# Flamingo block on one core: the drain of attention and GpSimd's queue reordered, the experts' bias added by VectorE

## The reference

```
x = x + tanh(g_xattn[0]) * cross_attention(layernorm(x), ctx)    # 32 q heads, 8 kv heads, head size 128, q and k rms-normed
x = x + tanh(g_ffn[0])   * per_head_ffn(layernorm(x))            # t = x[:, perm]; 16 heads: gelu(t_h @ up_h) @ down_h; inverse perm
x = x + tanh(g_xattn[1]) * group_attention(layernorm(x), ctx)    # att = sum(p * g) per group and block scales t; group norm; + ctx
x = x + tanh(g_ffn[1])   * routed_experts(layernorm(x))          # 8 experts 512 -> 512 with bias, each token takes its argmax expert
```

## Time and profile before

| | us |
|---|---|
| median of three runs | 793.2 |
| the three runs | 792.78, 793.2, 797.03 |
| the profiled execution | 797.66 |
| its span, first to last instruction | 795.9 |
| PE busy in the span | 755.1 (95%) |
| DVE, ACT, POOL busy | 459.6, 430.5, 274.5 |
| mean granted clock of PE | 0.982 of full |

### The profile page before, as it was taken

The page is one execution under the profiler, slowest core; times in us unless marked ns, Lnnn a source line. Parts: engine busy times, 40 slices in busy tenths (PEclk is TensorE's granted clock), DMA queues, the critical chain, the costliest instruction groups (busy, mean ns, idle before and its releaser), DMA issues.

```text
span 795.9 us, 12734 instructions
## 1 busy us (share of the span) xinstructions
PE 755.1 (95%) x3975; PEld 592.2 (74%) x3975; DVE 459.6 (58%) x1038; ACT 430.5 (54%) x1274; POOL 274.5 (34%) x431
## 2 busy tenths in 40 slices
PE   5999989899999999999999999999999987987997
PEld 3888877788888888888888888888887743555775
DVE  4786411556465656564655565656558764787652
ACT  4543315556556556555655655655555466557831
POOL 0331005234334233424423523433322438624242
PEclk9999999999999999999999999999999999797999
DMA  8545461132041140140131203203142135664232
GB/s 303 180 133 172 133 189 46 49 150 76 15 173 37 57 173 28 54 183 15 66 119 80 66 30 158 80 15 120 34 131 85 54 109 184 240 261 158 73 109 76
DMA packets 42126, 87.82 MB, mean 110 GB/s; under 512 B 5561, under 2 KB 26041, under 8 KB 38226
## 3 DMA queue, kind: packets, MB, share of 16 engines
q1 hardware_dynamic: 38884, 78.71, 28.7%
q0 software_dynamic: 3184, 8.41, 3.1%
HBM read 70.28 MB, written 35.57 MB: 133 GB/s over the span
## 4 chain that ended last, share of the span: by engine, by line
PE 71%; DVE 6%; ACT 3%; POOL 2%; DMA 2%; issue 1%; POOLq 0%; DVEq 0%; SPq 0%
PE banks L882 8%; PE banks L916 7%; PE banks L884 7%; PE banks L883 7%; PE banks L918 7%; PE banks L917 7%; PE banks L868 6%; PE banks L903 3%; PE banks L895 2%; PE banks L1831 2%; PE banks L1830 2%; PE banks L1832 2%; PE banks L927 2%; PE banks L929 2%; PE banks L928 2%
## 5 line engine op out<-in xcount | busy, mean ns | idle before, releaser
L592 ACT ACTIVATE p_sb<-p_sb,nmax 128x128 f32<-128x128 f32 x256 | 99.7, 391 | 62.7 <-DVE nmax L784 62.5
L587 ACT ACTIVATE oT_hi<-banks 128x512 fp32r<-128x512 f32 x64 | 38.2, 597 | 140.1 <-PE banks L929 140.1
L822 DVE SCALAR_TENSOR_TENSOR x_sb<-banks,tgates,x_sb 128x512 f32<-128x512 f32 x64 | 48.0, 749 | 70.8 <-PE banks L918 70.8
L690 POOL TENSOR_TENSOR v_lo<-v_raw,v_hi 128x128 fp32r<-128x128 f32 x64 | 29.5, 461 | 133.6 <-ACT v_hi L635 133.6
L779 DVE SCALAR_TENSOR_TENSOR p_sb<-banks,q_rstd,mask 128x128 f32<-128x128 f32 x256 | 71.5, 342 | 4.5 <-POOL q_rstd L83 4.0
L868 PEld LDWEIGHTS banks<-kT,qT_sb 128*128 128x128 f32 x512 | 67.7, 193 | 5.9 <-issue 0.5
L695 POOL TENSOR_TENSOR p_sb<-p_sb,rsum 128x512 f32<-128x512 f32 x64 | 66.5, 1040 | 15.2 <-DVE rsum L812 15.2
L868 PE MATMUL banks<-kT,qT_sb 128*128 128x128 f32 x512 | 68.2, 277 | 0.1
L768 DVE TENSOR_TENSOR oT_lo<-banks,oT_hi 128x512 fp32r<-128x512 f32 x64 | 44.1, 689 | 33.0 <-ACT oT_hi L587 33.0
L400 PE MATMUL banks<-w_hi,ctx_hi 128*128 128x512 f32 x128 | 54.1, 422 | 9.0 <-DVE ctx_lo L331 9.0
L816 DVE TENSOR_TENSOR pT_lo<-banks,pT_hi 128x512 fp32r<-128x512 f32 x64 | 44.2, 690 | 24.9 <-ACT pT_hi L610 24.9
(11 more groups left out here) (276 smaller groups left out, 1901.9 us busy)
## 6 DMA issues: line engine op xcount, KB each, us to landing
sorted_x<-in_empty SPq DMA_DIRECT2D x8, 2064.0 KB, 9.7
w_raw<-in_wq_l SPq DMA_DIRECT2D x8, 1024.0 KB, 5.1
w_raw<-in_wo_l SPq DMA_DIRECT2D x8, 1024.0 KB, 4.8
exp_w<-in_exp_w_l SPq DMA_DIRECT2D x8, 1024.0 KB, 9.3
kT_scr<-kT_st SPq DMA_DIRECT2D x16, 256.0 KB, 2.3
v_scr<-v_st SPq DMA_DIRECT2D x16, 256.0 KB, 2.3
xs<-sorted_x SPq DMA_DIRECT2D x15, 258.0 KB, 2.8
v_raw<-v_scr SPq DMA_DIRECT2D x14, 256.0 KB, 2.6
```

What stands on the lines that cost most here:

```text
L592: last = act.activation(p_sb[:, b % 2, h * P:(h + 1) * P], p_sb[:, b % 2, h * P:(h + 1) * P], ACT.Exp, bias=nmax[:, b % 2, h:h + 1], accum ...
```

## The change

1. In the drain PE does the first nine matmuls of the output projection (`o_first`, heads 0 to 2), then the values of the next unit, then the last three (`o_last`). `transpose_x` stands behind `o_last`. oT_hi and oT_lo become double buffers. The z product of block 4 moves from `middle` into step 65, ahead of `o_first`(63). The order on DVE and ACT stays.
2. On GpSimd all eight `scale_ctx` run before the second four gathers, once the shift of the second normalisation is known; then all twelve scatters follow without a break, then the clearing and `recycled`.
3. ACT loads the Gelu table before the second normalisation, not behind the copies of transposed x. PE's waits for those copies move from pack 0 to pack 1.
4. The bias is loaded broadcast (2 MB, `s.bias`), and DVE adds gate * bias to the row in each tile (`add_bias`, between `split_x` and `add_y`, with the expert's number read by DVE from t = 8). The bias matmul, the zeros, the splits and the stores of the bias go.
5. The remaining 16 chunks of weights are split three a tile, from tile 0 on.

```diff
@@ attention
-        oT_hi = m.sb("oT_hi", [P, D], F32R)
-        oT_lo = m.sb("oT_lo", [P, D], F32R)
+        oT_hi = m.sb("oT_hi", [P, 2, D], F32R)
+        oT_lo = m.sb("oT_lo", [P, 2, D], F32R)
...
             def oT_split(u, b, g, odd):
                 act.wait_ge(pv_done, u + 1)
-                reached(act, o_done, u)
-                act.activation(oT_hi[:, :], oT_ps[:, :], ACT.Copy).then_inc(oT_hi_done, 1)
+                reached(act, o_done, u - 1)
+                act.activation(oT_hi[:, b % 2, :], oT_ps[:, :], ACT.Copy).then_inc(oT_hi_done, 1)
...
+            def o_first(u, b, g, odd):
                 pe.wait_ge(oT_lo_done, u + 1)
                 reached(pe, acc_done, u - 1)
                 if after(u, b, g, B - 3):
                     pe.wait_ge(s.z_copied[1], 2)
+                o_heads(u, b, g, odd, range(HG - 1))
+
+            def o_last(u, b, g, odd):
+                o_heads(u, b, g, odd, (HG - 1,)).then_inc(o_done, 1)
...
+            def z4(u, b, g, odd):
+                if after(u, b, g, B - 1):
+                    pe.wait_ge(pT_lo_done, UNITS)
+                    z_product(4)
...
-                [(scores, 0), (sum_squares, 4), (z01, 0), (p_transpose, -1), (z2, -1), (o_proj, -2),
-                 (transpose_x, -4), (values, -1), (z3, -1)])
+                [(scores, 0), (sum_squares, 4), (z01, 0), (p_transpose, -1), (z2, -1), (z4, -2), (o_first, -2),
+                 (values, -1), (o_last, -2), (transpose_x, -4), (z3, -1)])
@@ middle, ACT
+            act.wait_ge(xseed_done, 2)
+            act.preload_act_table(ACT.Gelu)
             act.wait_ge(xshift_done, 1)
             normalise2(5)
             normalise2(7)
             copy_xT(5)
             copy_xT(7)
-            act.preload_act_table(ACT.Gelu)
@@ middle, GpSimd
                 if c:
                     pool.wait_ge(ctx_nat_ld, 16)
+                    pool.wait_ge(xshift_done, 1)
                     pool.wait_ge(col_step, 2)
-                    scale_ctx(range(2))
+                    scale_ctx(range(B))
...
-            scale_ctx(range(2, 4))
-            for jt in range(KT):
-                scatter(0, jt)
-                scale_ctx(range(4 + jt, 5 + jt))
+            for c in range(3):
+                for jt in range(KT):
+                    scatter(c, jt)
             nc.clear_and_free_semaphores(s.stage_sems)
             pool.memset(s.recycled_flag[:, :], 0.0).then_inc(s.recycled, 1)
-            for jt in range(KT):
-                scatter(1, jt)
-            for jt in range(KT):
-                scatter(2, jt)
@@ middle, PE
-            pe.wait_ge(xT_copied[0], 3)
-            pe.wait_ge(xT_copied[1], 5)
-            pe.wait_ge(z_copied[1], HB + 2)
...
-                            if k == 0 and i == 2:
-                                pe.wait_ge(z_copied[0], 2)
+                            if k == 0:
+                                pe.wait_ge(z_copied[i // 2 == 0], HB + 2 if i == 0 else 2)
+                            if k == 1 and i == 0:
+                                pe.wait_ge(xT_copied[0], 3)
+                                pe.wait_ge(xT_copied[1], 5)
@@ experts
+        def later_chunks(t):
+
+            return [divmod(c, KT) for c in range(READY * KT + 3 * t, min(READY * KT + 3 * t + 3, E * KT))]
...
-            sp.wait_ge(bias_zeroed, 1)
-            sp.dma_start(s.exp_b2[0:2, :, :].bitcast(F32), d.exp_b2).then_inc(exp_b_ld, 16)
+            sp.wait_ge(x3_done, B)
+            sp.dma_start(s.bias[:, :, :], d.exp_b).then_inc(bias_ld, 16)
...
-            run([(normalise, 2), (split_x, 1), (split_next_w, 3)])
+            run([(normalise, 2), (split_x, 1), (split_next_w, 1)])
...
+            def add_bias(t):
+                slot = t % SLOTS
+                dve.wait_ge(xn_done, t + 1)
...
+                    e = dve.value_load(tile_i[0:1, t - E:t - E + 1], min_val=0, max_val=E - 1)
+                dve.scalar_tensor_tensor(out=xs[:, slot, 0:D], in0=s.bias[:, e, :], scalar=s.tgates[:, 3:4],
+                                         in1=xs[:, slot, 0:D], op0=ALU.mult, op1=ALU.add).then_inc(bias_added, 1)
...
-            run([(split_x, 1), (add_y, -1), (split_next_w, 2)])
+            run([(split_x, 1), (add_bias, 1), (add_y, -1), (split_next_w, 0)])
...
-                pe.matmul(out, s.ones_r[:, :], s.exp_b2[:, e, :], start=True, stop=False)
```

More of the change, by code:

```diff
@@ L905, in p_transpose, with o_heads @@
                 last.then_inc(pT_done, 1)
-            def o_proj(u, b, g, odd):
+            def o_heads(u, b, g, odd, heads):
+                for h in heads:
+                    if b == 0:
+                        pe.wait_ge(wo_lo_done, 4 * g + h + 1)
+                    cols = slice(h * P, (h + 1) * P)
+                    oh, ol = oT_hi[:, b % 2, cols], oT_lo[:, b % 2, cols]
+                    pe.matmul(o_ps[b % 2][:, :], oh, wo_hi[odd][:, h, :], start=(h == 0), stop=False)
+                    pe.matmul(o_ps[b % 2][:, :], ol, wo_hi[odd][:, h, :], start=False, stop=False)
+                    last = pe.matmul(o_ps[b % 2][:, :], oh, wo_lo[odd][:, h, :], start=False, stop=(h == HG - 1))
+                return last
+            def o_first(u, b, g, odd):
                 pe.wait_ge(oT_lo_done, u + 1)
@@ L911, in o_proj @@
                     pe.wait_ge(s.z_copied[1], 2)
-                for h in range(HG):
-                    if b == 0:
-                        pe.wait_ge(wo_lo_done, 4 * g + h + 1)
-                    oh, ol = oT_hi[:, h * P:(h + 1) * P], oT_lo[:, h * P:(h + 1) * P]
-                    pe.matmul(o_ps[b % 2][:, :], oh, wo_hi[odd][:, h, :], start=(h == 0), stop=False)
-                    pe.matmul(o_ps[b % 2][:, :], ol, wo_hi[odd][:, h, :], start=False, stop=False)
-                    last = pe.matmul(o_ps[b % 2][:, :], oh, wo_lo[odd][:, h, :], start=False, stop=(h == HG - 1))
-                last.then_inc(o_done, 1)
+                o_heads(u, b, g, odd, range(HG - 1))
+            def o_last(u, b, g, odd):
+                o_heads(u, b, g, odd, (HG - 1,)).then_inc(o_done, 1)
+            def o_proj(u, b, g, odd):
+                pe.wait_ge(oT_lo_done, u + 1)
+                reached(pe, acc_done, u - 1)
+                o_heads(u, b, g, odd, range(HG)).then_inc(o_done, 1)
             def values(u, b, g, odd):
@@ L1384, in _ @@
             pe.wait_ge(s.gate_ld, 16 * GATE_LOADS)
-            pe.wait_ge(s.ones_set, 4)
+            pe.wait_ge(s.ones_set, 2)
             for kt in range(KT):
@@ L1536, in split_next_w @@
             def split_next_w(t):
-                if READY <= t < E:
-                    split_w(t)
-            run([(normalise, 2), (split_x, 1), (split_next_w, 3)])
+                for n, kt in later_chunks(t):
+                    e = ORDER[n]
+                    act.activation(s.ew_hi[:, e, kt, :], s.exp_w[:, e, kt, :], ACT.Copy).then_inc(w_hi_done, 1)
+            for e in range(HB):
+                act.wait_ge(s.exp_ld[e // 2], 32)
+            run([(normalise, 2), (split_x, 1), (split_next_w, 1)])
         @block.gpsimd
@@ L1829, in multiply @@
                     cols = slice(kt * P, (kt + 1) * P)
-                    pe.matmul(out, xsT_hi[:, t % 2, cols], s.ew_hi[:, e, kt, :], start=False, stop=False)
+                    pe.matmul(out, xsT_hi[:, t % 2, cols], s.ew_hi[:, e, kt, :], start=(kt == 0), stop=False)
                     pe.matmul(out, xsT_lo[:, t % 2, cols], s.ew_hi[:, e, kt, :], start=False, stop=False)
@@ L1938, in flamingo @@
             s.ctx_res, s.xln3, s.prod = beside("ctx_res", [P, B, D], 0), beside("xln3", [P, HB, D], 16), beside("prod", [P, 2, D], 24)
-            s.exp_b2, s.xn = beside("exp_b2", [P, E, D], 0, F32R), beside("xn", [P, 2, D], 24)
+            s.bias, s.xn = beside("exp_bias", [P, E, D], 0), beside("xn", [P, 2, D], 24)
             s.x3T = [s.at(f"x3T{c}", [P, KT, HALF], 8 * c) for c in range(2)]
```

65 lines of the change are left out of this document (22 added, 43 removed).

## The result

The changed kernel takes **801.25 us** (median of 6 runs, 799.63 to 803.94), the kernel before 793.62 us in the same job (6 runs): a ratio of 1.0095, 95% interval 1.0072 to 1.0117, 7.6 us slower. The forecast was 793.9 us, no change, with a range of 788.5 to 798.4: it was wrong. The profiled execution took 802.57 us, with a span of 800.8.

What follows compares the result with a forecast made beforehand. PE, busy 95% of the span, was taken as the bound; 797.7 + 4.4 - 0.25 - 3.65 - 4.5 + 0.2 = 793.9 us. From the 793.2 median without the -4.5 it was again 793.9; range 788.5 to 798.4.

Steps and rivals of the forecast that it cites:

- Part 1, the drain: In the drain, VectorE's order lengthens the steps, so the last accumulation comes 4.4 us later; bounds -2.4 to +6.
- rival (b): In the drain, PE's waits are covered as the order intends: -2.4 in place of +4.4, 787.1 us; 12%.
- Part 2: From the last unit to the gathers, moving scale_ctx away from the root gives -0.25 us, between -0.65 and +0.8.
- Part 3, the scatters: Before y, the fourth scatter comes 3.9 us earlier and the transposes of y follow: -3.65 us, other end 0.
- Part 4, the clock: In y, without an idle stretch ahead, PE's clock does not fall: -4.5 us, lower end 0.
- Rival (a): In the drain or at the start of y, the clock falls anyway: 798.4 us, slower; 15%.
- the two groups: Four times of the kernel before lie in two pairs, 792.8 and 793.2 against 797.0 and 797.7, separated by low clock.
- rival (d): In y, the median runs are like the profiled one and the pairs are chance: 789.4 us; 12%.
- Part 5, the experts: In the experts' tiles, VectorE's addition replaces PE's bias matmul and the rate stays: +0.2 us, between -3.5 and +3.
- the round: In the experts' tiles, the cycle result, store, load, normalise, split, next result: 9.82 us per three tiles, becoming 10.5.
- Rival (c): In the experts' tiles, PE stays the bound: -3.5 in place of +0.2, 790.2 us; 13%.
- Rival (e): In the experts' tiles, the result-to-result cycle with slow stores costs up to +3: 797 us; 8%.

Runs made afterwards that it cites:

- drain_stats_late: Kernel before with item 1 alone, plus VectorE's statistics of x moved one step later, behind pT_lo: 793.17 us, ratio 0.9985.
- before_again: The kernel before, unchanged, run once more for a second profile: 790.82 us.
- after_again: The changed kernel, unaltered, run once more for a second profile: 802.35 us.
- traffic: Kernel before with eight more 512 KB loads (4 MB in all) from SP's queue while the packs run: 798.42 us, one run.
- after_old_queue: Changed kernel with GpSimd's queue put back to the order of the kernel before: 798.98 us, ratio 1.0089.
- bias_behind: Kernel before with items 4 and 5 alone, but VectorE's add_bias placed behind add_y: 793.7 us, ratio 1.0000.
- best_a: Kernel before with statistics of x one step later, bias added by VectorE behind add_y, weights split two chunks a tile, two tiles ahead: 790.24 us, ratio 0.9934.
- The three parts alone: Kernel before with item 1 alone (799.55 us), with items 2 and 3 alone (796.09 us), and with items 4 and 5 alone (795.87 us).
- queue_only: Kernel before with items 2 and 3 alone (GpSimd's queue, the Gelu table and PE's waits): 796.09 us, ratio 1.0031.
- gap_scatters: Kernel before with items 2 and 3, but one scale_ctx behind each of the first three scatters: 795.04 us, ratio 1.0011.
- small_scatters: Kernel before with items 2 and 3, first four scatters cut to 16 KB each, first load of y from stored x: 794.68 us, one run.
- gap_gathers: Kernel before with items 2 and 3, but two scale_ctx between the last gather and the first scatter: 796.11 us, ratio 1.0024.
- gap_each: Kernel before with items 2 and 3, but one scale_ctx before each of the first four scatters: 795.32 us, ratio 0.9997.

## Why the prediction was wrong, by its steps

**Part 1, the drain: right.** +4.4 at the last accumulation, measured +4.4 in all four profiles with it, so rival (b) was out, with the forecast's marks (ring 6.36 for "close to 6.3"; wait for pT_lo 1.18; 646.2 for 646.3). drain_stats_late shows that the reason was the right one too: without the statistics between accumulate and oT_lo the loss is gone. The 5.5 that I expected of that run was too much by 1.2.

**Part 2: right in size.** From the last accumulation to the last gather 16.62 for 16.68, -0.06 where -0.25 was taken. The same stretch takes 15.50 in before_again, so -0.06 and -0.25 both lie inside what this stretch varies by itself.

**Part 3, the scatters: this step failed.** It says that "the whole 3.9 counts", because "PE's own work before them ends at 672.5 less 0.25 to 1". The scatters did move by 3.6. But the denser row, which the step took as free, makes PE's signals late and moves the end of the packs by 7.1 us against the last gather (6.4 in after_again), the low clock that follows in them included; the profiles of the old queue, traffic and its later packs aside, lie between 11.6 and 13.1, so the hold-up costs 5 to 7 us. In place of -3.65 the way to y measured +3.6 (+2.9). The reading error was to take the row's cost from GpSimd's timeline alone: each scatter costs 1.27 there. No row of before shows scatters in a row beside running packs; the earlier trace rows has them only from the end of the last pack on. That absence was a bound that the forecast should have named: the step had no upper end but 0.

**Part 4, the clock: right for y, wrong for the sum.** y takes 24.52 in place of 28.76, -4.2 for the forecast's -4.5, at the full level and without a wait before it, as the step said. But PE's wait in the packs put the low level there, 6.8 us of it. Rival (a) had the mechanism (the clock falls anyway), at 15%, with its place in the drain or at the start of y; the drain's waits of 1.2 us left the clock at 1.00. In the sum -4.5 was used once against the profiled 797.7, and the medians were left without it. before_again shows that a run even below the median has part of the fall. y takes 25.7 to 28.8 us in six of the nine profiles with the old GpSimd queue, behind waits of PE of 2.2 to 3.4. In two others (after_old_queue, drain_stats_late) the wait is as long, 3.56 and 2.97, the clock stays at 1.00, and y takes 24.5; so its length alone does not decide. The ninth, traffic, waits 0.46 and had its low level in the packs. Hence neither the two groups nor rival (d) was a true case, and the median lay in between. The Trainium skill, "TensorE: Matmul & The Clock Gate", part 1, says that where the clock changes differs between runs of one kernel; these profiles agree, and the pairs that I built on it do not exist.

**Part 5, the experts: too small.** +0.2 was taken, the tiles measured +2.2 (+3.9 in after_again). The step let "the rate stay" at 3.49 a tile through the round. It did not: of the 14 distances between tiles in the changed kernel six are 3.23 to 3.27, PE's own pace, my own sign of being wrong. The cost sits in others: in tiles 4 to 6 at 3.72 (the forecast's 3.75), where VectorE has no slack; at tile 8, where the experts' numbers begin to be read, 4.93 in place of 4.11; and at tiles 7, 11 and 13 with 4.13, 4.01 and 4.53 in place of 3.46. Ahead of each of those three ScalarE had waited for the load of the tile behind it (4.11, 2.46 and 4.83 us), whose slot comes free by the store six tiles before, thus for the round itself; and its split of tile 7, 11 or 13 stands behind that wait in its order. The last of them:

```profile
787.19 0.82 ACT L1520 ACTIVATE xn<-xs 128x512 f32<-128x512 f32 x1 [4.83 <-DMA xs<-sorted_x]
```

So, as I read it, PE runs ahead at its own pace until it meets the round. Rival (c), PE the bound, was right for single tiles, but what they gained was lost at the others. Rival (e), slower experts by the round, up to +3 at 8%, comes nearest. The loss of "about 2.5 us" in the first tiles was in my own text and was set against a gain that the round did not leave. bias_behind takes the addition out of the round and wins back 1.6, tile 11 among it (3.24). best_a has 3.23 to 3.26 in the first nine distances, and -1.55 in all.

**The sum**, stage by stage from the two first profiles: drain +4.4, way to y +3.6, y -4.2, from there to the tiles -0.4, tiles +2.2, tail -0.5, start and part 2 -0.1: +4.9, the difference of the spans. The medians differ by 7.6, that is 2.7 more, because the first profile of before lay 4.0 above its median and that of the changed kernel 1.3 above. The three parts alone cost 5.4, 2.0 and 1.7 us between the medians, 9.1 together; the 1.5 to the measured 7.6 is inside what the intervals leave open.

## What to carry to other kernels

When a change makes one engine's queue denser, look in the trace for a place where that density already stands beside the same neighbours; if there is none, the cost of it has an open upper end, whatever the queue's own rows say. After a reordering on the leading engine, follow each of its products to the queue that consumes them and move the work that stands in between there too: with PE's new order that made the difference between +4.4 and +0.1 us here. Then try that second move without the first: with PE's old order it gave -1.2. And profile the baseline more than once before a stage that varies by 4 us is given a term of its own.

## What was not expected of the hardware

In the kernel before a free VectorE starts its copy 0.07 us behind the end of the `down` product. Scatters issued by GpSimd 1.27 us apart hold up PE's completion signals to ScalarE and VectorE by 1.5 to 5.3 us: from the fifth indirect DMA in a row (changed, queue_only, gap_scatters, small_scatters) or about the third scatter on (gap_gathers, gap_each, traffic). The signal held longest comes 1.2 to 1.7 us after the end of the row's last issue (changed, after_again, queue_only, gap_gathers, small_scatters, traffic). 16 KB in place of 256 KB a scatter make no difference, 4 MB of other transfers do not cause it (one run each), and 2.0 us between the issues avoid it. Beside rows of four gathers a copy came 1.2 us late at most (best_a, 655.46). Signals of the others were on time: the scatter of 671.28 starts 0.28 us behind the end of VectorE's copy, and PE's `up` of 669.06 starts 0.05 behind the end of ScalarE's Gelu. Why PE's signals alone are late stays open; no run here tells.

The granted clock after a wait of 3 us before y varied between profiles of nearly equal kernels: 0.50 for 8 us in one (before), 1.00 throughout in two others (after_old_queue, drain_stats_late). Short falls of 3.4 us far ahead of the drain come in some executions of one kernel and not in others (two in before, none in before_again) and move its time by about 1.7 us each.
